# Four buffers instead of two for token rows and expert weights, loaded up to four jobs ahead, in a fused attention and mixture-of-experts kernel

## The reference, cut to what matters

```
h = layernorm(x) * (1 + ca) + sa
x = x + ga * attention(h)                 # scores get Q . rel_table[clip(j - i + 64, 0, 128)]
h = layernorm(x) * (1 + cb) + sb
logits  = silu(h @ rw1 + rb1) @ rw2 + rb2 # router: 128 -> 512 -> 8
k_prob  = softmax(top_2(logits))
for e in range(8):
    we  = sum(where(k_index == e, k_prob, 0))
    out += we * (silu(h @ w1[e] + b1[e]) @ w2[e] + b2[e])   # 128 -> 512 -> 128
return x + gb * out
```

## Time and profile before

| | |
|---|---|
| median of 3 runs | 733.77 us |
| the profiled execution | 733.48 us |
| its span from first to last instruction | 731.4 us |
| TensorE, busy | 601.9 us, 82% |
| ScalarE, busy | 572.6 us, 78% |
| VectorE, busy | 571.7 us, 78% |
| GpSimd, busy | 471.2 us, 64% |
| attention, up to the first job's load | 0 to 499 us |
| last parts of attention mixed with jobs 0 to 3 | 499 to 553.6 us |
| jobs 4 to 28 | 553.6 to about 694 us |
| results read back, weighted, stored | from 707.8 us |

### The profile page before, as it was taken

How to read it: one execution, slowest core, us unless ns; L and a number is a source line. 1 busy time by engine, 2 the same in 40 slices (tenths; PEclk the granted TensorE clock), 3 DMA queues, 4 the chain that set the end, 5 groups by cost and what they waited for, 6 DMA issues and landing times. The chain is left out here.

```text
span 731.4 us, 17828 instructions
## 1 busy us (share of the span) xinstructions
PE 601.9 (82%) x4964; PEld 450.1 (62%) x4964; DVE 571.7 (78%) x1980; ACT 572.6 (78%) x1710; POOL 471.2 (64%) x576
## 2 busy tenths in 40 slices
PE   5468888998898888989888889887776899999930
PEld 4345665665666656656655656554575789999830
DVE  5888988899989989989989989984745546666627
ACT  2059899898998998988989889897444768888824
POOL 2633755865878879778778797664546535565545
PEclk9769999999999999999999999999788989999975
DMA  5889788797887887888888878855348858888628
GB/s 151 245 225 270 239 271 265 231 281 239 239 275 228 264 269 237 260 267 239 267 244 262 261 232 274 256 177 178 94 121 245 263 174 274 280 267 277 233 72 274
DMA packets 183286, 172.25 MB, mean 235 GB/s; under 512 B 18115, under 2 KB 167396, under 8 KB 183190
## 3 DMA queue, kind: packets, MB, share of 16 engines
q1 hardware_dynamic: 177350, 161.75, 73.0%
q0 software_dynamic: 4832, 8.44, 3.4%
q10 hardware_dynamic: 1008, 0.93, 0.4%
HBM read 97.94 MB, written 74.63 MB: 236 GB/s over the span
## 5 line engine op out<-in xcount | busy, mean ns | idle before, releaser
L732 ACT ACTIVATE P<-NS,nmax 128x256 f32<-128x256 f32 x512 | 254.4, 506 | 22.8 <-DVE nmax L1382 19.6
L1382 DVE CUSTOM_DVE_ANT_0 NS<-psS,bias 128x256 f32<-128x256 f32 x512 | 185.3, 418 | 0.5 <-PE psS L1004 0.3
L1333 DVE COPY stage<-psDist 128x768 f32<-128x768 f32 x125 | 118.2, 946 | 41.7 <-PE psDist L963 13.5
L1022 PE MATMUL psT<-ident,P 128*128 128x128 f32 x1024 | 138.1, 278 | 14.4 <-ACT PT L743 14.4
L1022 PEld LDWEIGHTS psT<-ident,P 128*128 128x128 f32 x1024 | 115.8, 143 | 39.8 <-ACT P L732 22.3
L743 ACT ACTIVATE PT<-psT 128x512 f32<-128x512 f32 x256 | 136.6, 588 | 0.0
L639 POOL DMA_INDIRECT results_d<-y,row_u x87 | 86.1, 990 | 67.2 <-ACT y L796 48.1
L1520 DVE TENSOR_TENSOR FL<-F,FH 128x384 fp32r<-128x384 f32 x116 | 62.3, 558 | 52.5 <-ACT FH L810 52.3
L732 ACT ACTIVATION_READ_ACCUMULATOR P<-NS,nmax 128x1 f32 x512 | 101.1, 197 | 0.0
L802 ACT ACTIVATE F<-psS,b1T 128x384 f32<-128x384 f32 x116 | 66.1, 583 | 34.2 <-PE psS L1121 33.4
L1004 PE MATMUL psS<-Kst,Qst 32*128 32x256 f32 x512 | 65.8, 335 | 28.6 <-DVE nmax L1382 28.5
(11 more groups left out here) (263 smaller groups left out, 1299.5 us busy)
## 6 DMA issues: line engine op xcount, KB each, us to landing
dist_d<-stage SPq DMA_DIRECT2D x128, 384.0 KB, 3.2
bias<-dist_d SPq DMA_DIRECT2D x256, 192.0 KB, 3.4
wUp<-pairs_d SPq DMA_DIRECT2D x29, 512.0 KB, 4.5
wDown<-pairs_d SPq DMA_DIRECT2D x29, 512.0 KB
pairs_d<-pair SPq DMA_DIRECT2D x16, 512.0 KB, 4.3
x<-slots_d SPq DMA_DIRECT2D x29, 193.5 KB
raw<-in_L_ffn_w_dram SPq DMA_DIRECT2D x16, 256.0 KB, 4.5
y<-results_d SPq DMA_DIRECT2D x16, 256.0 KB, 5.3
```

The lines of the kernel that those rows point to most:

```text
L732: act.activation(P[:, p % 2, h, q, :], NS[:, p % 2, h, q, :], ACT.Exp, scale=-1.0, bias=nmax[:, p % 2, k:k + 1], accum_out=lsum[:, b % 2, ...
L1022: mm = pe.transpose(psT[:, h, S * k + 128 * q:S * k + 128 * q + 128], P[:, p % 2, h, q, 128 * k:128 * k + 128], ident[:])
L1333: dve.tensor_copy(stage[:, p % STAGES, :, :, :], bank[:, :, 0:2 * RW].rearrange("p h (q c) -> p h q c", q=2)).then_inc(dist_out, 1)
L1382: dve.tensor_tensor_reduce(NS[:, p % 2, h, q, :], psS[:, h, S * q:S * q + S], bias[:, p, h, q, :], 1.0, 3e38, ALU.add, ALU.min, nmax[:, p ...
```

## The change

`wUp`, `wDown` and `x` get four buffers each (`DEEP`), and job j uses number j modulo 4. `wUp` and `wDown` take the 32 KB of each partition that the attention's `bias` ring had, `y1` and `y2` are put at the same addresses as the weights, and `x` and the tiles behind it move up by as much. Each of the three loads of job j waits for the use of the buffer by job j - 4 instead of job j - 2. SyncE's order is written anew: `load_x(j)`, `load_up(j)`, `load_down(j - 1)` in every place, where it was x(j), up(j - 1), down(j - 2). One wait is added, for the last maximum of the attention (`max_done`), ahead of up(1).

```diff
+DEEP = 4
...
-        x = t("x", [128, 2, EK, ROW])
-        wUp = t("wUp", [128, 2, 2, HID], FR)
-        wDown = t("wDown", [128, 2, 2, HID], FR)
+        with ExitStack() as weight_tiles:
+            wUp = weight_tiles.enter_context(nc.sbuf_tensor("wUp", [128, DEEP, 2, HID], FR))
+            wDown = weight_tiles.enter_context(nc.sbuf_tensor("wDown", [128, DEEP, 2, HID], FR))
+        y1 = t("y1", [128, TT, E])
+        y2 = t("y2", [128, TT, E])
+        x = t("x", [128, DEEP, EK, ROW])
...
             def load_x(j):
-                past(sp, x_turned, j - 1)
-                past(sp, rows_known, j - 1)
+                past(sp, x_turned, j + 1 - DEEP)
+                past(sp, rows_known, j + 1 - DEEP)
...
-            def load_w(j, n, w, used, count, arrived):
+            def load_up(j):
                 e = of_tile(sp, j)
-                past(sp, used, count)
+                past(sp, up, HK * (j + 1 - DEEP))
...
+            def load_down(j):
+                e = of_tile(sp, j)
+                past(sp, down, j + 1 - DEEP)
...
             sp.wait_ge(planned, 1)
-            load_w(0, 0, wUp, up, 0, up_in)
+            load_up(0)
             for k in range(RINGS):
                 sp.wait_ge(sent[k], 16 * 4 * KNOWN // RINGS)
             load_x(0)
-            load_w(0, 1, wDown, down, 0, down_in)
             load_x(1)
-            for n, w, arrived in ((0, wUp, up_in), (1, wDown, down_in)):
-                load_w(1, n, w, up, 0, arrived)
-            for j in range(2, FULL + 1):
-                if j == FULL - 2:
+            sp.wait_ge(max_done, 4 * STEPS)
+            load_up(1)
+            load_down(0)
+            load_x(2)
+            load_up(2)
+            load_down(1)
+            for j in range(3, JOBS):
+                if j == FULL - 1:
                     sp.wait_ge(consts_done, 1)
                     sp.dma_start(slots_d[UNUSED:UNUSED + ET, :].rearrange("(p k) e -> p k e", p=128),
                                  fill[:]).then_inc(filled, 16)
                     pad(sp, range(EXP // 2))
-                if j < FULL:
-                    load_x(j)
-                if 2 <= j - 1:
-                    load_w(j - 1, 0, wUp, up, HK * (j - 2), up_in)
-                if 2 <= j - 2:
-                    load_w(j - 2, 1, wDown, down, j - 3, down_in)
-            sp.wait_ge(planned, 2)
-            load_w(FULL, 0, wUp, up, HK * (FULL - 1), up_in)
-            load_w(FULL - 1, 1, wDown, down, FULL - 2, down_in)
-            for k in range(RINGS):
-                sp.wait_ge(sent[k], 16 * 4 * B // RINGS)
-            sp.wait_ge(filled, 16 * (EXP + 1))
-            load_x(FULL)
-            load_x(FULL + 1)
-            for j in range(FULL + 2, JOBS + 2):
-                if j < JOBS:
-                    load_x(j)
-                if j - 1 < JOBS:
-                    load_w(j - 1, 0, wUp, up, HK * (j - 2), up_in)
-                load_w(j - 2, 1, wDown, down, j - 3, down_in)
+                if j == FULL:
+                    sp.wait_ge(planned, 2)
+                    for k in range(RINGS):
+                        sp.wait_ge(sent[k], 16 * 4 * B // RINGS)
+                    sp.wait_ge(filled, 16 * (EXP + 1))
+                load_x(j)
+                load_up(j)
+                load_down(j - 1)
+            load_down(JOBS - 1)
```

More of the change, by code:

```diff
@@ L318, in attention @@
         gbR = t("gbR", [B, E])
-        y1 = t("y1", [128, TT, E])
-        y2 = t("y2", [128, TT, E])
         def pt(name, shape):
@@ L370, in attention @@
         gates_turned, gates_out, gates_wide = sm("gates_turned"), sm("gates_out"), sm("gates_wide")
-        x_in = [sm("x_in0"), sm("x_in1")]
-        up_in = [sm("up_in0"), sm("up_in1")]
-        down_in = [sm("down_in0"), sm("down_in1")]
+        x_in = [sm(f"x_in{k}") for k in range(DEEP)]
+        up_in = [sm(f"up_in{k}") for k in range(DEEP)]
+        down_in = [sm(f"down_in{k}") for k in range(DEEP)]
         x_turned, x_high, x_low, rows_known = sm("x_turned"), sm("x_high"), sm("x_low"), sm("rows_known")
@@ L382, in arrivals @@
         def arrivals(j):
-            return 16 * (j // 2) + 16
+            return 16 * (j // DEEP) + 16
         def gate(b, n):
@@ L464, in load_x @@
             def load_x(j):
-                past(sp, x_turned, j - 1)
-                past(sp, rows_known, j - 1)
+                past(sp, x_turned, j + 1 - DEEP)
+                past(sp, rows_known, j + 1 - DEEP)
                 n = sp.value_load(firstrow[0:1, j:j + 1], min_val=0, max_val=UNUSED)
-                sp.dma_start(x[:, j % 2, :, :], slots_d[bass.ds(n, ET), :].rearrange(
-                    "(p k) e -> p k e", p=128)).then_inc(x_in[j % 2], 16)
-            def load_w(j, n, w, used, count, arrived):
+                sp.dma_start(x[:, j % DEEP, :, :], slots_d[bass.ds(n, ET), :].rearrange(
+                    "(p k) e -> p k e", p=128)).then_inc(x_in[j % DEEP], 16)
+            def load_up(j):
                 e = of_tile(sp, j)
-                past(sp, used, count)
-                sp.dma_start(w[:, j % 2, :, :].bitcast(FP), pairs_d[bass.ds(e, 1), n].rearrange("a p s h -> p (a s) h"))\
-                    .then_inc(arrived[j % 2], 16)
+                past(sp, up, HK * (j + 1 - DEEP))
+                sp.dma_start(wUp[:, j % DEEP, :, :].bitcast(FP),
+                             pairs_d[bass.ds(e, 1), 0].rearrange("a p s h -> p (a s) h")).then_inc(up_in[j % DEEP], 16)
+            def load_down(j):
+                e = of_tile(sp, j)
+                past(sp, down, j + 1 - DEEP)
+                sp.dma_start(wDown[:, j % DEEP, :, :].bitcast(FP),
+                             pairs_d[bass.ds(e, 1), 1].rearrange("a p s h -> p (a s) h")).then_inc(down_in[j % DEEP], 16)
             sp.wait_ge(planned, 1)
-            load_w(0, 0, wUp, up, 0, up_in)
+            load_up(0)
             for k in range(RINGS):
@@ L1093, in turn_x @@
             def turn_x(j):
-                pe.wait_ge(x_in[j % 2], arrivals(j))
+                pe.wait_ge(x_in[j % DEEP], arrivals(j))
                 past(pe, x_high, j)
@@ L1098, in turn_x @@
                 for k in range(EK):
-                    mm = pe.transpose(psX[:, 128 * k:128 * k + 128], x[:, j % 2, k, 0:E], ident[:])
+                    mm = pe.transpose(psX[:, 128 * k:128 * k + 128], x[:, j % DEEP, k, 0:E], ident[:])
                 mm.then_inc(x_turned, 1)
@@ L1112, in go_up @@
                 if k == 0:
-                    pe.wait_ge(up_in[j % 2], arrivals(j))
+                    pe.wait_ge(up_in[j % DEEP], arrivals(j))
                     pe.wait_ge(x_low, j + 1)
@@ L1118, in go_up @@
                 out = psH[:, k % 2, 0:ET]
-                pe.matmul(out, wUp[:, par, 0, at], xH[:, par, :], start=True, stop=False)
-                pe.matmul(out, wUp[:, par, 0, at], xL[:, par, :], start=False, stop=False)
-                pe.matmul(out, wUp[:, par, 1, at], xH[:, par, :], start=False, stop=True).then_inc(up, 1)
+                pe.matmul(out, wUp[:, j % DEEP, 0, at], xH[:, par, :], start=True, stop=False)
+                pe.matmul(out, wUp[:, j % DEEP, 0, at], xL[:, par, :], start=False, stop=False)
+                pe.matmul(out, wUp[:, j % DEEP, 1, at], xH[:, par, :], start=False, stop=True).then_inc(up, 1)
             def go_down(j, k):
                 if k == 0:
-                    pe.wait_ge(down_in[j % 2], arrivals(j))
+                    pe.wait_ge(down_in[j % DEEP], arrivals(j))
                     past(pe, y_biased, j)
@@ L1129, in go_down @@
                 out = psE[:, 0:ET]
-                pe.matmul(out, wDown[:, par, 0, at], FH[:, par, k, :], start=(k == 0), stop=False)
-                pe.matmul(out, wDown[:, par, 0, at], FL[:, par, k, :], start=False, stop=False)
-                mm = pe.matmul(out, wDown[:, par, 1, at], FH[:, par, k, :], start=False, stop=(k == HK - 1))
+                pe.matmul(out, wDown[:, j % DEEP, 0, at], FH[:, par, k, :], start=(k == 0), stop=False)
+                pe.matmul(out, wDown[:, j % DEEP, 0, at], FL[:, par, k, :], start=False, stop=False)
+                mm = pe.matmul(out, wDown[:, j % DEEP, 1, at], FH[:, par, k, :], start=False, stop=(k == HK - 1))
                 if k == HK - 1:
@@ L1510, in split_x @@
                 past(dve, up, HK * (j - 1))
-                dve.tensor_copy(row_u[:, j, :], x[:, j % 2, :, E:ROW].rearrange("p k a -> p (k a)"))\
+                dve.tensor_copy(row_u[:, j, :], x[:, j % DEEP, :, E:ROW].rearrange("p k a -> p (k a)"))\
                     .then_inc(rows_known, 1)
```

## The result

The changed kernel takes 724.3 us, the median of four runs (723.44 to 725.33); the kernel before, on the same chip in the same rounds, 732.55 us. The ratio is 0.988, with a 95% interval from 0.9835 to 0.9924. The forecast was 726.0 us, 723.0 to 730.6.

A forecast was written before the change was run, and what follows sets the result against it. The prediction took TensorE as the bound, so a load landing earlier helps only where TensorE stands still for it. 6.9 us (x(9)) plus 0.6 us (small waits) is 7.5 us: 733.5 - 7.5 = 726.0 us, range 723.0 to 730.6.

The forecast's parts named there:

- The wait for x(9): Job 8: TensorE's wait for late token rows goes entirely and the job falls from 12.05 us; gain 6.9 us.
- 2.44 us for the clock: Job 8 from its transposes on: 6.45 us at mean clock 0.56 against job 7's 4.01 at 1.00, part of the 6.9.
- the second rival: Near the boundary: idle time goes but TensorE's clock falls elsewhere; gain only 4.6 us, 728.9 us; chance 0.12.
- The small waits: Steady stretch: three waits for wUp go because up(j) is asked for earlier; gain 0.6 us.
- the upper bound I had (0.97): Steady stretch: all that 19 jobs take beyond 5.03 us each, 96.54 - 95.57 = 0.97 us.
- What costs nothing: Unchanged load count and bytes, the added max_done wait, first loads, shared transfer engines and SBUF room: no cost charged.
- The slower rival: Start, 499 to 524 us: the first burst of loads delays engine code; four pieces caught give 744.4 us; chance 0.05.
- The first rival: ScalarE's fill stretch: table reads get 1.2 us shorter and all 0.97 us goes; gain 9.1 us, 724.4 us; chance 0.10.

The follow-up runs named there:

- layout: Kernel before with the changed kernel's tile addresses and added wait, still two buffers used and the old order: 734.22 us, ratio 0.9995.
- x9_first: Kernel before, two buffers, with x(9) asked for ahead of up(9) and down(8): 728.98 us, ratio 0.9913 to before.
- pads_sync_two: Kernel before, two buffers, with ScalarE's four fills given to SyncE, which then asks for all eight: 736.91 us, ratio 1.0039 to before.
- late_x9: Changed kernel with x(9), and all SyncE asks for behind it, held until job 8's first block is over: 727.83 us, ratio 0.993 to before.
- two_ordered: Kernel before, two buffers, x(9) ahead of up(9) and down(8), and up(j - 1) ahead of x(j) in every place: 723.76 us, ratio 0.9883.
- hold_early: Changed kernel, four buffers, but loads 0 to 3 wait as with two buffers, so without the burst at the start: 725.04 us, one run.
- pads_sync: Changed kernel with ScalarE's four fills given to SyncE, which then asks for all eight: 720.15 us, ratio 0.9797 to before.
- pieces_spread: pads_sync with x(8) ahead of the fills, token count earlier, VectorE's second table in eight pieces at parts 29 and 33 to 49: 715.46 us, ratio 0.9775.

## Why the prediction was right

**The wait for x(9).** Forecast: asked for at 567.4, no wait, 6.9 us. Measured: 567.34, no wait, 6.91 us. With the trace's 2.44 us for the clock the sum gave 6.9. The estimate by the rule of the Trainium skill ("TensorE: Matmul & The Clock Gate", Terms) was 2.8 us for the clock, and the gain by it 7.3; here the durations of the trace were the better price. The clock is 1.00 from job 5 through job 27, so the second rival (2.4 us paid elsewhere) did not come.

**The small waits.** This term was mis-sized: 0.6 us taken, from the three waits that the list names, and 0.94 measured, which is the upper bound I had (0.97). The list names the stops that it can put down to a load, and the stretch loses more than these. TensorE's products are busy for all of the 96.54 us, and still 0.94 us went: the three named waits are those of its weight loads, so a full busy share did not prove that nothing was lost. In three other kernels with the old order in these jobs (layout, x9_first, pads_sync_two) the same 19 jobs took 97.67 to 97.94 us, one execution each. Against those the term is worth up to 2.3 us, and the one profiled execution of before was a kind one.

**Why it works.** The prediction saw that x(9) stood 14 us behind loads whose buffers were not free, and then credited the cure to buffers. late_x9 shows that the wait is what costs; x9_first and two_ordered show that order alone removes it. So the number was right and the credit was not: the change moved the order together with the buffers, and the order is enough. That holds for the weights too: the prediction named x(j + 1) in front of up(j), and then counted only the buffer.

**What costs nothing.** Addresses, added wait (layout), burst (hold_early, queue of code): nothing that can be seen, as charged. The slower rival is out; the first transposes' 0.84 us are within the scatter of attention.

**The first rival** (ScalarE's table reads get shorter) came in part: the long read was 1.51 us in before and is 1.28 in after, and job 4 is 0.25 us shorter. That stretch moves by itself: job 4 took 11.82 and 11.60 us in two executions of the changed kernel, and 9.51 in hold_early, with TensorE's wait between 2.0 and 4.5 us. Of it nothing can be credited to the change.

**Sum.** 7.5 us forecast against 8.15 between the two profiled executions. 0.34 of the difference is the small-wait term; the other 0.3 is the balance of the other stretches, which moved by up to 0.84 us each and nearly cancelled. That the sum came out so close is in part luck: job 4 alone differs by 2.3 us between hold_early and after. The median of after's four runs is 1.0 us below its profiled one, so against 726.0 the measured time is 1.7 us lower.

## What to carry to other kernels

A late load's cost is read from when it was asked for and from what stood in front of it in the asking stream, before any thought of more buffers: here moving a few lines gave with two buffers all that four gave. More buffers may be worth their room when the asking stream itself will be kept busy for longer than a job, as by the eight fills; that was not tried against the better order with two. And when a wait is removed, the next one to look at is where another engine's stream asks for transfers in the middle of its arithmetic: that was worth 5.2 us in job 4, three quarters of what job 8 gave.

## What the runs showed of the hardware

- The landing of the same 193.5 KB depends on what is under way ahead of it: 3.88 us with down(8) 1.3 us in front of it, 2.56 us when SyncE had asked for nothing in the 16 us before (late_x9). In after, where a weight load stands close in front of most x, the median of the 29 landings is 4.1 us.
- Asking is not free. Each fill, with its table read, keeps the asking engine for 1.1 to 1.3 us on the mean: eight took 10.01 us on SyncE in pads_sync and 8.97 in pieces_spread, and moving four of them off ScalarE shortened job 4 from 11.8 to 6.6 us.
- After TensorE had stood for 2.93 us its granted clock was 0.50 from 584 to 586 us and 1.00 from 588 to 590 (late_x9), with TensorE busy throughout. From the transposes on, job 8 took 5.43 us there where a plain job takes 4.01, so the clock took about 1.4 us; by the same measure it took 2.44 after the longer stop of before (4.3 us).
- The steady jobs need 0.81 to 0.89 of the transfer engines' time in different kernels (after and two_ordered) at the same 5.03 to 5.04 us a job, so there the transfer engines did not set the time. A stretch of two microseconds ran at 407 GB/s (late_x9).
